# A fused attention and mixture-of-experts block on one core: ScalarE's root of the variance behind the first Ln, down projections in whole experts between pairs of scores, query, key and value copies on VectorE, values projected before the last weighted values

## The reference, cut to what matters

```
x = x + attn(layernorm(x))
    # s = q k^T / 4;  s = s - max(s);  w = 1/(1 - s(1 - s/2 (1 - s/3)));  out = (w / sum w) v, times w_out, + b_out
x = x + ffn(layernorm(x))
    # logits = x router_w + router_b;  p = softmax(logits);  gates = the 2 largest of 4, divided by their sum
    # h_e = silu(x w1_e) * (x w3_e);  out = sum over e of gates_e * (h_e w2_e)
```

## Time and profile before

| what | us |
|---|---|
| median of 3 runs (lowest, highest) | 1249.19 (1246.94, 1249.32) |
| the profiled execution's own time | 1247.45 |
| its span | 1245.4 |

### The profile page before, as it was taken

The page is one execution under the profiler, slowest core; times in us unless marked ns, Lnnn a source line. Parts: engine busy times, 40 slices in busy tenths (PEclk is TensorE's granted clock), DMA queues, the critical chain, the costliest instruction groups (busy, mean ns, idle before and its releaser), DMA issues.

```text
span 1245.4 us, 29490 instructions
## 1 busy us (share of the span) xinstructions
PE 1112.9 (89%) x10116; PEld 975.4 (78%) x10116; DVE 960.7 (77%) x1774; ACT 1031.1 (83%) x1102; POOL 740.0 (59%) x963
## 2 busy tenths in 40 slices
PE   2569999999999999999999999999999999999988
PEld 1447888888877888887788888778888877888877
DVE  5768788888778888877888887788888778888732
ACT  2488988888898888889888888988888898888862
POOL 6116556666655666665566666556666655666555
PEclk9878999999999999999999999999999999999989
DMA  5112211222211122221112222111222221122000
GB/s 172 62 61 73 67 59 51 78 82 81 80 61 59 49 76 81 81 81 61 57 50 76 81 81 81 61 56 51 76 81 81 75 66 54 53 76 78 29 23 26
DMA packets 92906, 84.89 MB, mean 68 GB/s; under 512 B 11784, under 2 KB 87240, under 8 KB 92872
## 3 DMA queue, kind: packets, MB, share of 16 engines
q1 hardware_dynamic: 92296, 83.92, 21.0%
q10 hardware_dynamic: 576, 0.52, 0.2%
HBM read 62.20 MB, written 21.10 MB: 67 GB/s over the span
## 4 chain that ended last, share of the span: by engine, by line
POOL 32%; issue 20%; PE 20%; DMA 12%; DVE 9%; SPq 2%; ACT 2%; POOLq 1%; DVEq 0%
POOL hid L396 25%; DMA gate_all<-gate_scratch 9%; PE up L828 6%; PE up L1000 5%; DVE mx L714 5%; POOL xn L429 4%; DMA gate_scratch<-gates 2%; PE sc L984 1%; PE sc L894 1%; ACT poly L550 1%; PE misc L1045 1%; PE pv L844 1%; PE misc L1018 1%; SPq L324 1%; PE misc L1053 1%
## 5 line engine op out<-in xcount | busy, mean ns | idle before, releaser
L396 POOL TENSOR_TENSOR hid<-hid,gate_all 128x512 f32<-128x512 f32 x256 | 410.2, 1618 | 130.2 <-DVE hid L624 75.1
L632 DVE SCALAR_TENSOR_TENSOR poly<-w_sq,sc 128x1024 f32<-128x1024 f32 x256 | 309.1, 1218 | 94.9 <-ACT w_sq L488 88.0
L488 ACT ACTIVATE w_sq<-sc 128x1024 f32<-128x1024 f32 x256 | 259.5, 1027 | 109.1 <-PE sc L894 108.1
L714 DVE TENSOR_REDUCE mx<-sc 128x4 f32<-128x1024 f32 x256 | 304.8, 1215 | 56.5 <-PE sc L984 56.5
L1000 PE MATMUL up<-w_sb,hid 128*128 128x128 f32 x2048 | 256.2, 279 | 0.6 <-POOL hid L396 0.6
L550 ACT ACTIVATE poly<-poly,two 128x2048 f32<-128x2048 f32 x128 | 252.0, 1992 | 0.4
L828 PE MATMUL up<-xn_hi,w_hi 128*128 128x256 f32 x832 | 245.9, 296 | 1.6 <-DVE y_acc L727 1.1
L1000 PEld LDWEIGHTS up<-w_sb,hid 128*128 128x128 f32 x2048 | 240.0, 193 | 8.5 <-POOL hid L396 0.8
L555 ACT ACTIVATE poly<-poly 128x2048 f32<-128x2048 f32 x128 | 242.5, 1895 | 0.0
L828 PE MATMUL up<-xn_hi,w_lo 128*128 128x256 f32 x832 | 234.4, 282 | 0.0
L828 PE MATMUL up<-xn_lo,w_hi 128*128 128x256 f32 x832 | 233.7, 281 | 0.0
(11 more groups left out here) (98 smaller groups left out, 1416.2 us busy)
## 6 DMA issues: line engine op xcount, KB each, us to landing
qk_scratch<-qk_split SPq DMA_DIRECT2D x32, 512.0 KB, 2.9
k_pad<-qk_scratch SPq DMA_DIRECT2D x256, 64.0 KB
gate_all<-gate_scratch SPq DMA_DIRECT2D x32, 512.0 KB, 3.9
q_stack<-qk_scratch SPq DMA_DIRECT2D x124, 128.0 KB
x_in<-in_L_attn_x_dram SPq DMA_DIRECT2D x32, 128.0 KB, 2.1
x_res<-in_L_attn_x_dram SPq DMA_DIRECT2D x32, 128.0 KB, 2.3
out_dram<-y_acc SPq DMA_DIRECT2D x32, 128.0 KB, 2.3
poly<-in_L_ffn_w_dram SPq DMA_DIRECT2D x2, 1024.0 KB, 6.8
```

Source lines behind the costliest of these rows:

```text
L396: nc.gpsimd.tensor_tensor(h, h, by_token.unsqueeze(1).to_broadcast([128, 2, C, 128]), ALU.mult).then_inc(gated, 1)
L488: nc.scalar.activation(w_sq[:, u % 2, :], sc[:, u % 2, :], ACT.Square).then_inc(sq_ok, 1)
L632: nc.vector.scalar_tensor_tensor(poly[:, u, :], w_sq[:, u % 2, :], 3.0, sc[:, u % 2, :], ALU.add, ALU.mult).then_inc(poly_ok, 1)
L714: nc.vector.tensor_reduce(by_row[:, :, 2 * g:2 * g + 2], sc[:, u % 2, :].rearrange("p (j k t) -> p j k t", j=2, k=2), AX.X, ALU.min, negat ...
```

## The change

On ScalarE the second Ln goes behind the root of the variances. On GpSimd the eighth gating unit goes from the end of the first half to a place behind `half_var`. The copies of `qk` and `v_pad` go from ScalarE to VectorE: the first to the start of its first half, the second ahead of `hidden(0)`, with the waits that they had. TensorE projects the values ahead of the last weighted values. Its order of down projections and scores becomes one whole expert and then two scores, four times. VectorE's `router_T` and `experts_added` go ahead of the seventh maximum, and its `route_logits` and `compare` behind `maxima_out`; TensorE's `router_logits` goes between the two up projections of unit 0 and waits for `m_ok`; the waits that guard `misc` change with the order.

```diff
 (GpSimd, first_half)
-                    for u in range(UP):
-                        ... (wait hid_ok, gate the unit)
+                    for u in range(UP - 1):
+                        gate_hidden(m, u)
 (GpSimd, second_half, behind half_var)
+                if has(i, off - 2):
+                    gate_hidden(no(i, off) - 2, UP - 1)
+                if lo < hi:
                     pool.wait_ge(rstd0_ok, k + 1)
 (ScalarE, first_half)
-                    nc.scalar.copy(qk[:], misc[:]).then_inc(qk_out, 1)
...
-                    after(act, pv_full, G * (m - 1))
-                    for c in range(C):
-                        last = nc.scalar.copy(v_pad[par][:, c, :, 16:16 + HD], ...
 (ScalarE, second_half)
                     log_of(0)
-                    log_of(1)
...
-                    if has(i, off) and 0 < g < G - 1:
+                    if has(i, off) and g < G - 1:
                         log_of(g + 1)
 (VectorE, first_half)
+                if has(i, off + 1):
+                    m = n + 1
+                    dve.wait_ge(qk_full, m + 1)
+                    after(dve, qk_ok, m)
+                    nc.vector.tensor_copy(qk[:], misc[:]).then_inc(qk_out, 1)
+                def values_copied():
+                    m, par = n + 1, (off + 1) % 2
+                    dve.wait_ge(v_full, m + 1)
+                    after(dve, pv_full, G * (m - 1))
+                    nc.vector.tensor_copy(v_pad[par][:, :, :, 16:16 + HD], ...).then_inc(v_ok, 1)
                 for u in range(U):
+                    if u == 0 and has(i, off + 1):
+                        values_copied()
                     if u == 0 and has(i, off - 2):
                         hidden(0)
 (VectorE, second_half)
                 for u in range(U):
+                    if u == 6 and has(i, off - 1):
+                        router_T()
+                    if u == 6 and has(i, off - 2):
+                        experts_added()
                     if has(i, off + 1):
                         scores_max(u)
-                    (router_T behind maximum 4; route_logits and experts_added behind maximum 6)
                 if has(i, off + 1):
                     split_maxima()
+                    maxima_out()
                 if has(i, off - 1):
+                    route_logits()
                     compare()
-                (maxima_out)
 (TensorE, first_half)
                 distance(0)
                 distance(1)
-                (weighted_values 3)
                 (values, which wait for qk_out)
+                (weighted_values 3)
                 ups(1)
 (TensorE, second_half)
-                down(0, (0,))
+                down(0)
                 score(0)
                 score(1)
-                down(0, (1,))
                 down(1)
...
                 down(3)
-                    router_logits()
                 score(6)
                 score(7)
...
                     up_a_unit(i, off - 1, 0)
+                    router_logits()
                     up_b_unit(i, off - 1, 0)
 (guards of misc)
-                        pe.wait_ge(lg_ok, n)
+                        pe.wait_ge(xn2_out, n)      # maxima_T
+                        pe.wait_ge(lg_ok, n)        # queries_operand
+                        pe.wait_ge(m_ok, n + 2)     # router_logits
```

More of the change, by code:

```diff
@@ L374, in _, with gate_hidden @@
             blank_stacks(pool, 0)
+            def gate_hidden(m, u):
+                pool.wait_ge(hid_ok, UP * m + u + 1)
+                h = hid[:, 2 * u:2 * u + 2, :].rearrange("p k (c t) -> p k c t", c=C)
+                by_token = gate_all[:, :, :, 2 * u // FB].rearrange("p t c -> p c t")
+                nc.gpsimd.tensor_tensor(h, h, by_token.unsqueeze(1).to_broadcast([128, 2, C, 128]),
+                                        ALU.mult).then_inc(gated, 1)
             def first_half(i, off):
@@ L515, in first_half @@
                     nc.scalar.copy(o_T[:], pv[:]).then_inc(o_ok, 1)
[L516 to L519, removed]
-                    after(act, pv_full, G * (m - 1))
-                    for c in range(C):
-                        last = nc.scalar.copy(v_pad[par][:, c, :, 16:16 + HD],
-                                              misc[:, c * D:(c + 1) * D].rearrange("p (h d) -> p h d", d=HD))
-                    last.then_inc(v_ok, 1)
                 silu(1)
@@ L639, in first_half @@
                     split_w3()
+                if has(i, off + 1):
[7 more added lines that the diff above has]
+                    after(dve, pv_full, G * (m - 1))
+                    nc.vector.tensor_copy(v_pad[par][:, :, :, 16:16 + HD],
+                                          misc[:, 0:C * D].rearrange("p (c h d) -> p c h d", c=C, d=HD)).then_inc(v_ok, 1)
                 def normalized():
@@ L790, in second_half @@
                 for u in range(U):
+                    if u == 6 and has(i, off - 1):
+                        router_T()
+                    if u == 6 and has(i, off - 2):
+                        experts_added()
                     if has(i, off + 1):
                         scores_max(u)
[L793 to L798, removed]
                 if has(i, off + 1):
                     split_maxima()
+                    maxima_out()
                 if has(i, off - 1):
+                    route_logits()
                     compare()
-                if has(i, off + 1):
-                    maxima_out()
                 if has(i, off + 2):
@@ L811, in _ @@
             dve.wait_ge(consts_ok, 4)
+            dve.wait_ge(consts_v, 4)
             over_batches(dve, first_half, second_half)
@@ L912, in first_half @@
                 distance(1)
-                if has(i, off - 1):
-                    weighted_values(i, off - 1, 3)
                 if has(i, off + 1):
@@ L921, in first_half @@
                     last.then_inc(v_full, 1)
+                if has(i, off - 1):
+                    weighted_values(i, off - 1, 3)
                 ups(1)
@@ L1024, in queries_operand @@
                     pe.wait_ge(xn_ok, m + 1)
-                    if has(i, off + 1):
+                    if has(i, off - 1):
+                        pe.wait_ge(lg_ok, n)
+                    elif has(i, off + 1):
                         pe.wait_ge(m_ok, n + 2)
-                    elif has(i, off - 1):
-                        pe.wait_ge(lg_ok, n)
                     for c in range(C):
@@ L1050, in router_logits @@
                     pe.wait_ge(xn2_out, m + 1)
+                    if has(i, off + 1):
+                        pe.wait_ge(m_ok, n + 2)
                     for c in range(C):
```

## The result

The changed kernel takes 1283.01 us (median of 4 runs, 1281.74 to 1284.51); the kernel before takes 1248.61 beside it. The ratio is 1.0278, with a 95% interval of 1.026 to 1.0296: slower by 34 us. The forecast was 1257, slower, with a range to 1272. The direction holds, and so does the mechanism (the copy of the values holds back VectorE's queue); the size does not. The profiled execution took 1284.51 us (span 1282.8), against 1247.45 (span 1245.4).

The account below looks back on a forecast made before the run. No engine is full; a loop of waits closing each 36.38 us cycle bounds the kernel. Loss 1.97 less gain 1.66 is 0.31 us, times 30 cycles is 9 us on 1247.45: said 1257, range 1236 to 1272.

Parts of the forecast that it names:

- T: Start of the maxima's transposes on TensorE in each cycle; forecast at 684.53, a gain of 1.66 us.
- The second half: Stretch up to the maxima's transposes: down(0) waits for silu 7, yet the transposes come 1.66 us sooner.
- The root: Root of the variances, before Newton on GpSimd: 1.3 us sooner, but only removes TensorE's wait; the maxima are late next.
- The way from T: From the maxima's transposes to up_b_unit(2): grows from 9.17 to 11.14 us, 1.97 more.
- four gate steps 0.85: VectorE's gate steps between the end of the ranks and the copy of qk: 0.85 us in all.
- the one branch: Logits, comparisons, ranks and gate steps before the copy of qk: T + 4.8, beside queries and keys at T + 4.70.
- net of 0.31 us: Change per cycle: 1.97 lost on the way from the maxima's transposes against 1.66 gained before them.
- The values' copy: On VectorE it waits for pv_full, with hidden(0), polynomials 0 and 1 and hidden(1) queued behind; polynomial 0 at 692.64, was 692.07.
- 1.0 us of cover: ScalarE's stall for shifted makes square 0 end at 691.6, while polynomial 0 starts only at 692.64 for VectorE's sake.
- the third: Rival: slower by much, from a costlier copy of qk or longer logits' way; 1266, or 1273 with the copy's long end; chance 0.14.
- The faster rival: Maxima come sooner because VectorE's 0.97 us idle before maxima 0, 2, 4 shrinks; 1242, or 1228 without any; chance 0.24.
- The rule of the Trainium skill: Next VectorE operation waits for an empty pipe; four joints from values' copy to hidden(1) add 0.35 us a cycle, 10 us.

Follow-up runs that it names:

- e4: Kernel before plus only the second Ln behind the variances' root and the eighth gating unit behind half_var: 1221.97 us, ratio 0.9797.
- e8: Kernel before with the root's part alone, plus VectorE's experts' sum and logits' three steps ahead of the seventh maximum: 1207.97 us, ratio 0.9676.
- e3: Changed kernel with GpSimd's addition of bias to residual moved from behind the ranks to ahead of the router's operand: 1275.98 us, ratio 1.0234.
- e2: Changed kernel with the values' copy moved on VectorE from ahead of hidden(0) to behind hidden(1): 1245.90 us, ratio 0.999.
- e1: Changed kernel with TensorE doing the last weighted values ahead of the values' projection again: 1272.34 us, ratio 1.0206.
- e5: Changed kernel with the logits' Exp moved on ScalarE behind the last Exp of the weights: 1281.77 us, ratio 1.0264.
- e6: Changed kernel with its first half as before (both copies on ScalarE, last weighted values ahead of values): 1258.17 us, ratio 1.0082.
- e7: Changed kernel with VectorE's copy of qk ahead of the four gate steps instead of behind them: 1269.72 us, ratio 1.0175.

## Why the prediction was right in direction and wrong in size

**The cycle and its two ways.** Right: the loss is in the cycle, and the cycle is the second half's way to T plus the way from T. The cycle before was put at 36.38 and is 36.33.

**The second half.** Right: the gain was put at 1.66 us including the 0.35 that `down(0)` waits for silu 7. Measured from T to T it is 1.95 for the stretch from the first down projection, where the forecast has 15.58 - 13.57 = 2.01. The root, priced as only removing a wait of TensorE, gives 0.89 us of it (e4). The text said that the maxima are late next; they are, and e8 shows it by moving what stood between them, for 0.58. The other 1.06 of the change come with the new order on TensorE and VectorE; no run has the whole experts on TensorE alone, so what that part is worth stays open.

**The way from T.** This is where the size failed. The forecast amounts to a first down projection at T + 23.06: 20.74 as before, 1.97 that the way grows, and 0.35 for silu 7. It came at T + 23.80. The 0.74 us are made of these terms:

| term | forecast | measured | what it is |
|---|---|---|---|
| T to the copy of qk | 4.80 | 5.33 | 0.23 a gate step stretched by GpSimd (e3), 0.21 half of a loop turn of 0.42, the rest small |
| copy of qk to the values | 0.77 | 0.75 | |
| values to weighted values | 0.47 | 0.64 | TensorE; the forecast's rows have an up projection behind the values |
| weighted values to the values' copy | 1.13 | 1.14 | |
| the copy to `hidden(1)` | 3.23 | 3.20 | |
| `hidden(1)` to the first down projection | 12.66 | 12.74 | |

The largest part is the first row, the copy of `qk` at T + 4.8, and in it the step "four gate steps 0.85" is the mis-sized term. From the end of the ranks (T + 4.05, put at 3.95) to the copy (T + 5.12) the changed kernel takes 1.07 us even without the turn. I took the steps from rows in which the first of them had no GpSimd addition beside it for its length, because VectorE reached it late. Once the step waits for the ranks, it starts with the addition that GpSimd does behind the ranks. The second omission is the turn of VectorE's loop, 0.42 us in every second cycle. It was in the trace before, under a wait for ScalarE, and the text looked at one kind of cycle only:

```profile
689.94 0.69 DVE L624 TENSOR_TENSOR hid<-silu_a,up 128x512 f32<-128x512 f32 x1 [0.49 <-ACT silu_a L496]
```

Silu 0 ends at 689.43 in this cycle, half a microsecond before VectorE starts. Both costs lie on the one branch that the text called equal to the other (T + 4.70 and T + 4.8): where two branches tie, any small cost on either is paid in full. The third term is the 0.17 by which the weighted values start later behind the values than an up projection does in the earlier trace rows. The forecast's net of 0.31 us was the difference of 1.97 and 1.66, so an error of 0.8 us in a way of 23 made it 1.11.

**The count of cycles.** The sum took 30 cycles and expected little of the filling and draining ones. Between the first and the last transposes the loss is 30.4 us in place of 9, but the drain adds 6.7 in the profiled execution, which the sum had at nothing. Part of that is ScalarE's stall, which has no cover there.

**The values' copy.** Right, and the part that decides: the copy waits for `pv_full` and holds back `hidden(0)`, both polynomials and `hidden(1)`. Its wait is 1.83 us, and e2 takes 1.30 us off the cycle by moving it alone. e1 shows that projecting the values sooner does not help but costs 0.41. The copy of `qk` was put at 0.69 and takes 0.69.

**ScalarE.** Right: a stall of 1.28 to 1.39 us was put at 1.2, with 1.0 us of cover. e5 removes the stall and the cycle does not move. e6 takes the cover away, and the forecast of 1257 stands against 1258.

**The rivals.** The nearest to what happened is the third: the logits' way longer than T + 4.8. It was priced at 9 us for each 0.3 us and had a chance of 0.14; the way came to 0.53 more, of which 0.21 is the loop's turn that it did not name, with 0.17 beside it on TensorE that no rival had. The faster rival failed at its condition: the three idle times of VectorE are there (0.38, 0.29, 0.36 against 0.33, 0.32, 0.32). The rule of the Trainium skill (VectorE: DVE Perf Modes, on the DRAIN), by which four joints would add 0.35 us, did not come true: from the copy to `hidden(1)` it took 3.20, where the forecast without the rule had 3.23. The same section adds that a next operation that is not held starts earlier, and here it does: `hidden(0)` ends at 674.05, polynomial 0 starts at 673.97.

## What to carry to other kernels

A copy that is moved to another engine takes its waits with it: ask what stands behind it in the new queue, and not only how long it takes. Test the parts of a bundle one by one: here the root (with the gating unit's move) gains 2.0% alone, and the rest of the bundle turned that into a loss of 2.8%. Where a forecast is the small difference of two large sums, or two branches tie, put the range by the sums.

## What the runs showed of the hardware

A VectorE step over 8 elements with two inputs in SBUF takes 0.16 us, but 0.40 us when a GpSimd operation on SBUF runs beside it. In the changed kernel it starts at 669.47 and ends at 669.88; the first of GpSimd's two additions runs from 669.40 for 0.45. In e7 the same happens to another step: `gates` (also two tensor inputs) takes 0.64 and ends at 628.52, beside this row of GpSimd, which ends at 628.50:

```profile
627.46 1.04 POOL L389 TENSOR_TENSOR qk_split<-qk,zero 128x512 fp32r<-128x512 f32 x1 [0.77 <-DVE qk L807]
```

The step beside it with one input (`chosen_r`, 0.17) was not stretched. In the kernel before, the gate step starts at 688.61 beside the last 0.08 us of GpSimd's additions (687.82 to 688.69) and keeps its 0.16. So in these runs the short operation ends only when the GpSimd operation has ended. The profile's times on GpSimd are rough; that the addition causes the stretch rests on e3, where it is moved away. The Trainium skill (GPSIMD Engine Reference, section on the specifications) says that GpSimd's SBUF interfaces are shared with VectorE and that instructions with two SBUF inputs contend; these rows agree.

The order of values (weights of 128 columns) and weighted values (weights of 32) is not neutral on TensorE: 1.64 us from the first's start to the next work in the one order, 1.47 in the other. Why is open; no run took it apart. For the values' copy the two orders are equal within 0.05 us (e1).
